# GNN pair kernel: layer 1 one group later, P ahead of K V, P turned through DRAM, five x slots

## The reference

```python
h = relu(layernorm(x))
z_l, z_g, v = h @ W_lang.T, h @ W_grav.T, h @ W_V.T
zn  = z_l / max(norm(z_l), 1e-8)
A_l = max(zn @ zn.T, 0) * not_eye
A_g = exp(-max(|z_g,n - z_g,m|^2, 0) / (2 sigma^2)) * not_eye
K   = w_l * rowstochastic(A_l * adj) + (1 - w_l) * rowstochastic(A_g * adj)
x   = x + (K @ v) @ W_O.T                 # layer 0
h   = relu(layernorm(x))
x   = x + einsum('bnf,nm->bmf', h, adj * adj) + bias   # layer 1
```

## Time and profile before

| | |
|---|---|
| median of 3 runs | 1266.11 us |
| profiled execution | 1266.65 us |
| its span, first to last instruction | 1264.8 us |
| mean granted TensorE clock | 0.994 |
| PE busy | 1241.4 us, 98% |
| DVE busy | 1058.7 us, 84% |
| ACT busy | 694.6 us, 55% |
| POOL busy | 575.5 us, 46% |

### The profile page before, as it was taken

One profiled execution on the slowest core, in us unless ns is written; L12 is line 12 of the kernel. 1 busy time (PEld: TensorE's weight loads), 2 busy tenths in 40 slices (PEclk: granted clock), 3 DMA queues, 4 the chain that ended last, 5 costly groups with the idle time before them and its releaser, 6 DMA issues.

```text
span 1264.8 us, 22572 instructions
## 1 busy us (share of the span) xinstructions
PE 1241.4 (98%) x6324; PEld 1039.9 (82%) x6324; DVE 1058.7 (84%) x1826; ACT 694.6 (55%) x1324; POOL 575.5 (46%) x964
## 2 busy tenths in 40 slices
PE   7999999999999999999999999999999999999996
PEld 7888888888888888888888888888888888888884
DVE  5688888898888898888898888898888898888777
ACT  6346655456655546655546655545655545664543
POOL 1124554434554434555444555444555343455433
PEclk9999999999999999999999999999999999999997
DMA  6233333443333444242444242444242334243201
GB/s 243 34 76 87 96 76 73 100 108 93 89 84 65 100 108 99 84 97 53 100 107 104 79 107 47 100 103 106 79 106 58 91 100 108 81 102 72 45 34 66
DMA packets 308894, 112.55 MB, mean 89 GB/s; under 512 B 269840, under 2 KB 269968, under 8 KB 308880
## 3 DMA queue, kind: packets, MB, share of 16 engines
q1 hardware_dynamic: 177360, 95.78, 27.6%
q10 hardware_dynamic: 131520, 16.60, 8.0%
HBM read 46.20 MB, written 33.62 MB: 63 GB/s over the span
## 4 chain that ended last, share of the span: by engine, by line
PE 92%; DVE 5%; issue 2%; ACT 1%; DMA 0%; DVEq 0%; ACTq 0%
PE ring L868 73%; PE p_ps L868 15%; PE p_ps L941 2%; PE kt_ps L881 1%; PE ring L958 1%; DVE x_out L689 1%; DVE y_lo L558 1%; PE p_ps L967 0%; DVE deg L603 0%; DMA x_ring<-in_L_gnn_W_lang 0%; DVE h L573 0%; DVE chain L587 0%; ACT v_hi L442 0%; DVE K L617 0%; ACT h L379 0%
## 5 line engine op out<-in xcount | busy, mean ns | idle before, releaser
L301 POOL TENSOR_TENSOR x_out<-x_ring,bias_sb 128x512 f32<-128x512 f32 x128 | 162.7, 1293 | 498.9 <-DVE bn L638 498.9
L406 ACT ACTIVATE y_hi<-ring 128x512 fp32r<-128x512 f32 x256 | 148.4, 593 | 201.8 <-PE ring L868 199.0
L868 PE MATMUL ring<-hT_hi,Lw_hi 128*128 128x512 f32 x640 | 256.4, 401 | 2.1 <-DVE hT_lo L577 1.3
L868 PE MATMUL ring<-hT_hi,Lw_lo 128*128 128x512 f32 x640 | 250.1, 391 | 0.0
L868 PE MATMUL ring<-hT_lo,Lw_hi 128*128 128x512 f32 x640 | 249.8, 390 | 0.0
L558 DVE TENSOR_TENSOR v_lo<-ring,v_hi 128x512 fp32r<-128x512 f32 x128 | 88.4, 692 | 137.2 <-ACT v_hi L442 137.2
L868 PE MATMUL ring<-MT_hi,hT_hi 128*128 128x512 f32 x512 | 202.6, 396 | 0.0
L868 PE MATMUL ring<-MT_lo,hT_hi 128*128 128x512 f32 x512 | 199.6, 390 | 0.0
L868 PE MATMUL ring<-MT_hi,hT_lo 128*128 128x512 f32 x512 | 199.6, 390 | 0.0
L308 POOL TENSOR_TENSOR h_lo<-h2f,h_hi 128x512 fp32r<-128x512 f32 x124 | 158.0, 1295 | 85.1 <-ACT h_hi L476 85.1
L558 DVE TENSOR_TENSOR y_lo<-ring,y_hi 128x512 fp32r<-128x512 f32 x256 | 168.8, 679 | 26.4 <-ACT y_hi L406 26.4
(11 more groups left out here) (160 smaller groups left out, 2539.6 us busy)
## 6 DMA issues: line engine op xcount, KB each, us to landing
x_ring<-in_x SPq DMA_DIRECT2D x32, 1024.0 KB, 5.5
out<-x_out SPq DMA_DIRECT2D x128, 256.0 KB, 2.2
h_turned<-h SPq DMA_DIRECT2D x248, 64.0 KB, 2.1
h_turned<-h ACTq DMA_DIRECT2D x248, 64.0 KB, 2.1
rn_cols<-rn_dram SPq DMA_DIRECT2D x31, 256.0 KB, 3.8
x_ring<-in_L_gnn_W_lang SPq DMA_DIRECT2D x4, 256.0 KB, 5.2
h2f<-in_L_gnn_W_grav SPq DMA_DIRECT2D x1, 1024.0 KB, 8.9
chain<-in_L_gnn_W_O SPq DMA_DIRECT2D x1, 1024.0 KB, 12.8
```

Of the source, the lines that this page charges most:

```text
L301: pool.tensor_tensor(x_out[:, b], x_rows(g, b), bias_sb[:, :], ALU.add).then_inc(x2b_ready, 1)
L406: act.activation(y[0][:, a, :, l], bank(n).rearrange("p (b m) -> p b m", b=GB), ACT.Copy)\
L868: mm = pe.matmul(out, lhsT, rhs, start=(k == 0), stop=(k == len(terms) - 1))
```

## The change

Diff line numbers are left out; "..." marks lines that are not shown. It does these things:

- P stands directly behind the y blocks and K's transposes, with its loop over a outside the loop over elements, and K V behind P. K's transposes stand behind the eighth y block instead of the seventh.
- The eight transposes of P on PE are gone, except in the last group. DVE transposes P's 32x32 blocks (`turn_p`, two operations), SP stores them to DRAM (two DMAs), and eight DMAs fetch them to their places in P_turned, which lies in the tile of h. S is then two adds in the next iteration (`sum_s`), behind the third y_lo, and mask, exponentials, row factors and the combination follow later in that iteration.
- The scaling by the norms and the mask are one operation on DVE; the product of spread norms and mask is made by POOL (`mask_norms`).
- Layer 1 of a group is computed an iteration later, with h2's hi and lo parts and the bias. x_out is gone: bias and output are added into x itself, which keeps five slots instead of four.
- All 16 DMAs of the turned h are issued by SP; ACT issues none in the loop. The second pair of block transposes stands behind the eighth y_lo.
- The statistics of the residual stand behind the lo parts of the first two elements of hT; all four `h2_full` stand at the end of ACT's iteration.

```diff
-SLOTS = 4
+SLOTS = 5
...
+            def store_p(g, l):
+                sp.wait_ge(p_blocks, 2 * g + l + 1)
+                sp.dma_start(p_dram[l], P_blocks[:, l].rearrange("p j b q -> p j (b q)")).then_inc(p_stored[l], 16)
+
+            def fetch_p(g, l):
+                sp.wait_ge(p_stored[l], 16 * g + 16)
+                for j in range(NQ):
+                    sp.dma_start(P_turned[j * Q:(j + 1) * Q, l], p_dram[l][:, j].rearrange("(i r) e -> r i e", r=Q))\
+                      .then_inc(p_turned[l], 16)
+
+            def spread_norms_turn_p(g):
                 sp.wait_ge(rn_step, RN_STEPS * g + 1)
                 sp.dma_start(rn_dram, rn[:, 0]).then_inc(rn_stored, 16)
                 sp.wait_ge(rn_stored, 16 * g + 16)
                 sp.dma_start(rn_cols[:, :, :], rn_dram.unsqueeze(0).to_broadcast([P, P, GB])).then_inc(rn_spread, 16)
+                store_p(g, 0)
+                store_p(g, 1)
+                fetch_p(g, 0)
+                fetch_p(g, 1)
 
             def turn_h(g):
                 sp.wait_ge(blocks_ready, GB * g)
-                for i in range(NQ // 2):
+                for i in range(NQ):
                     for j in range(NQ):
                         sp.dma_start(turned_to(i, j), h_blocks[i * Q:(i + 1) * Q, j]).then_inc(turned, 16)
 
-            def iteration(i, load=True, after=True):
-                if after:
-                    turn_h(i + 1)
-                if after:
-                    spread_norms(i)
-                store_out(i - 1, first_use(i) + PER - GB)
+            def iteration(i, load=True, lag=True):
                 if load:
-                    sp.wait_ge(x_loaded, 16 * i + 48)
-                    load_x(i + 3)
+
+                    sp.wait_ge(out_stored, 16 * GB * (i - 2))
+                    load_x(i + 2)
+                turn_h(i + 1)
+                spread_norms_turn_p(i)
+                if lag:
+                    store_out(i - 2, first_use(i) + PER - GB)
...
+            def mask_norms(g):
+                pool.wait_ge(rn_spread, 16 * g + 16)
+                pool.wait_ge(p_stored[0], 16 * g + 16)
+                by_row = mask[:, :].unsqueeze(1).to_broadcast([P, GB, P])
+                pool.tensor_tensor(rn_mask, rn_cols[:, :, :].rearrange("p m b -> p b m"), by_row, ALU.mult)\
+                    .then_inc(rn_masked, 1)
...
-            def iteration(i, before=True, after=True):
+            def iteration(i, before=True, lag=True, after=True):
                 if after:
                     norm1(i + 1)
+                if lag:
+                    for b in range(GB):
+                        h2_lo(i - 2, b)
+                    for b in range(GB):
+                        add_bias(i - 2, b)
+                row_norms(i)
                 if before:
-                    for b in range(GB // 2):
-                        add_bias(i - 1, b)
                     norm2(i - 1)
-                if not after:
-                    row_norms(i)
-                if before:
-                    for b in range(GB // 2, GB):
-                        add_bias(i - 1, b)
                 if after:
-                    row_norms(i)
-                if before:
-                    for b in range(GB):
-                        h2_lo(i - 1, b)
+                    mask_norms(i)
...
+                        act.wait_ge(s_ready, 2 * g - 2)
...
-            def turn_h(g):
-                act.wait_ge(blocks_ready, GB * g)
-                for i in range(NQ // 2, NQ):
-                    for j in range(NQ):
-                        act.dma_start(turned_to(i, j), h_blocks[i * Q:(i + 1) * Q, j]).then_inc(turned, 16)
 
...
-                        if after and 3 <= n < 5:
-                            normalize(i + 1, (n - 3) * GB // 2)
-                        if before and n == 4:
+                        if before and n == 3:
+                            exponentials(i - 1)
+                        if after and n == 5:
+                            normalize(i + 1, 0)
+                        if before and n == 6:
                             w_g_K_g(i - 1)
-                        if before and n == G_USES - 1:
-                            kt_copy(i - 1)
-                if after:
-                    turn_h(i + 1)
+                        if after and n == 7:
+                            normalize(i + 1, GB // 2)
+                if lag:
+                    for b in range(GB):
+                        h2_copy(i - 2, b)
+                if before:
+                    kt_copy(i - 1)
+                    act.wait_ge(s_ready, 2 * i)
+                for half in range(2):
+                    act.wait_ge(p_done, GB * i + 2 * half + 2)
+                    act.activation(P_sb[:, 2 * half:2 * half + 2], p_ps[:, 2 * half:2 * half + 2], ACT.Copy)\
+                       .then_inc(p_copied, 1)
+                if not after:
+                    shift(i)
...
-                    act.wait_ge(s_ready, i)
-                    act.wait_ge(diag_ready, 2 * i)
-                for half in range(2):
-                    act.wait_ge(p_done, GB * i + 2 * half + 2)
-                    act.activation(P_sb[:, 2 * half:2 * half + 2], p_ps[:, 2 * half:2 * half + 2], ACT.Copy)\
-                       .then_inc(p_copied, 1)
-                if not after:
-                    shift(i)
-                if before:
-                    h2_full(i - 1, 0)
-                    h2_full(i - 1, 1)
...
-                    if before and b == 0:
-                        h2_copy(i - 1, 0)
-                        h2_copy(i - 1, 1)
                     if b == 0 and after:
                         shift(i)
-                    if before and b == 1:
-                        h2_full(i - 1, 2)
-                    if before and b == 2:
-                        h2_full(i - 1, 3)
-                        h2_copy(i - 1, 2)
-                        h2_copy(i - 1, 3)
-                if after:
-                    exponentials(i)
+                if not after:
+                    kt_copy(i)
+                if before:
+                    for b in range(GB):
+                        h2_full(i - 1, b)
+                        if not after:
+                            h2_copy(i - 1, b)
...
             def mask_l(g):
-                dve.wait_ge(a_ready, 3 * g + 1)
+                dve.wait_ge(rn_masked, g + 1)
+                dve.wait_ge(s_ready, S_STEPS * (g + 1))
+                dve.scalar_tensor_tensor(out=A[:, :, 0], in0=A[:, :, 0], scalar=0.0,
+                                         in1=rn_mask,
+                                         op0=ALU.max, op1=ALU.mult).then_inc(a_ready, 1)
...
+            def output_bias(g, b, n):
+                dve.wait_ge(l1_done, GB * g + b + 1)
+                dve.wait_ge(h2_done, GB * g + b + 1)
+                dve.tensor_tensor(x_rows(g, b), x_rows(g, b), bias_sb[:, :], ALU.add).then_inc(x2b_last, 1)
+                dve.wait_ge(x2b_last, b + 1)
+                dve.tensor_tensor(x_rows(g, b), bank(n), x_rows(g, b), ALU.add).then_inc(drained, 1)
...
-                        if before and n == 1:
+                        if before and n == 3:
+                            sum_s(i - 1, 1)
+                            sum_s(i - 1, 0)
+                            mask_l(i - 1)
+                        if before and n == 4:
                             mask_g(i - 1)
-                        if before and n == 2:
                             row_factors(i - 1)
-                        if after and n == 4:
+                        if before and n == 6:
+                            combine(i - 1)
+                        if after and n == 6:
                             turn_blocks(i + 1, 0)
                             turn_blocks(i + 1, 1)
-                        if before and n == 4:
-                            combine(i - 1)
-                        if after and n == 5:
-                            turn_blocks(i + 1, 2)
-                            turn_blocks(i + 1, 3)
-                        if before and n == G_USES - 1:
-                            kt_lo(i - 1)
+                if after:
+                    turn_blocks(i + 1, 2)
+                    turn_blocks(i + 1, 3)
+                    if x_next:
+                        x_stats(i + 2, 0, GB)
+                if not after:
+                    last_chain(i, n, use, hi)
+                    return
                 if before:
-                    residual(i - 1, n, first_use(i) + n, i + 2 if stats and after else None)
+                    kt_lo(i - 1)
+                    add(i - 1, 0, n)
+                    add(i - 1, 1, n + 1)
+                squared_norms(i)
+                if before:
+                    add(i - 1, 2, n + 2)
+                    add(i - 1, 3, n + 3)
...
                     turned_lo(i + 1, b)
-                    if b == (2 if before else GB - 1):
-                        sum_s(i)
-                if before:
+                    if before and b < GB // 2:
```

(69 more changed lines are left out.)

## The result

The changed kernel takes **1283.53 us** (median of 4 runs, 1282.72 to 1283.90) against 1266.11: ratio 1.0136, 95% interval 1.0119 to 1.0154, slower by 1.4%. Its profiled execution took 1283.9 us with a span of 1282.1, clock 0.991.

A forecast was written before the change was run, and what follows sets the result against it. A ring of waits, 38.0 us a group, was taken to bound the changed kernel: 28 x 0.27 = 7.6, head 1.5, tail 4, so +13.1 us and 1279 us. Range 1248 to 1302, the forecast's own 1268 to 1292.

The forecast's parts named there:

- The ring: Loop's closed chain of waits through DVE, SP's DMAs, ACT and GpSimd: 38.0 us a group, 1.1 more than PE needs.
- the ends: Work outside the repeating groups: head +1.5 us (group 0's y to group 1's), tail +4 us behind the last K V.
- The transposes: Eight fp32 transposes of P on PE, removed in 31 of 32 groups: 0.87 us a group, leaving PE 36.86.
- rival 1: Turned h not late, TensorE stays the bound: 24.4 us go, ends cost 5.5, 1247 us, chance 0.16.
- (1): DVE from the first y_lo to the last block transpose: 13.3 us.
- (2): Turning h through 16 DMAs issued by SP alone, from turned blocks to turned h: 12.15 us.
- (3): ACT's hT_hi of the first element, behind the turned h: 0.62 us.
- (4): DVE's hT_lo, statistics, v_lo, second hT_lo and two more statistics: 4.3 us.
- (5): norm2 on GpSimd, from its first operation to the normalization it releases: 3.9 us.
- (6): Four h2f on ACT and the first y_hi, which releases the next y_lo: 3.45 us.
- six hand-overs of 0.05: Waits between the ring's steps, about 0.05 us each, added to their sum of 37.7 to give 38.0 us.
- rival 3: DVE's added strided operations and the fetches cost their upper ends: 38.9 us a group, 1304 us, chance 0.16.

The follow-up runs named there:

- h: Changed kernel with the residual's statistics two places earlier on DVE and GpSimd's product of norms and mask behind the next group's first norm: 1248.89 us.
- l: h with the last two block transposes also moved ahead of the eighth y_lo: 1245.93 us, ratio 0.9840.
- g: Old kernel without the turning of P (computes another matrix, only its time is of use): 1267.25 us, ratio 1.0008.
- d: Changed kernel with the last two block transposes ahead of the eighth y_lo: 1262.93 us, ratio 0.9977.
- e: Changed kernel with the last two block transposes behind the four statistics of x: 1370.97 us, ratio 1.0830.
- k: Changed kernel with six more small GpSimd multiplications ahead of the second norm's factors: 1340.01 us, ratio 1.0582.
- j: Changed kernel with only GpSimd's product of norms and mask moved behind the next group's first norm: 1282.78 us, ratio 1.0132.
- c: Changed kernel with only the residual's statistics moved two places earlier on DVE: 1286.20 us, ratio 1.0161.
- a: Changed kernel with ACT again issuing 8 of the 16 DMAs that turn h: 1267.37 us, ratio 1.0010.
- i: Changed kernel, last group only: GpSimd's factors ahead of its bias additions, each h_lo behind one output_bias on DVE: 1283.70 us, ratio 1.0141.
- section 4: Experiment on the changed kernel that moved statistics and mask product singly and together (c, j, h); its table lists landmark times from a group's first layer 1 output.

## Why the prediction came out right

It said 1279 us and slower; 1283.5 lies within the forecast's own range. The ring is shown by the runs. That the number came so close is in part luck, as the ends below tell.

**The transposes, 0.87 us a group: about right for PE, wrong as a gain that the old kernel could have taken.** The 36.86 us that I gave PE alone were passed in h and l (36.77 and 36.71, at 1248.9 and 1245.9 us). PE's busy time in a group fell by 1.16 us, from 37.68 to 36.52 in h, and not by 0.87: the V stage lost 0.93 us with the transposes, and the y stage 0.39 (14.14 to 13.75, means over groups 3 to 31), where I had put K's transposes and the new order at equal cost. That is rival 1, 1247 us, as a kernel: it needed the ring gone, as the text said. But g shows that in the old kernel nothing of it was to be had.

**The ring, step by step: confirmed.** From the rows above: (1) 573.39 to 586.65, 13.26 us, forecast 13.3. (2) to hT_hi at 598.88, 12.23, forecast 12.15. (3) 0.67, forecast 0.62. (4) 599.55 to 603.90, 4.35, forecast 4.3. (5) to 607.83, 3.93, forecast 3.9. (6) to the next y_lo at 611.28, 3.45, forecast 3.45. Sum 37.89, where the mean period is 37.88. My 38.0 came from six hand-overs of 0.05 put on top of 37.7; steps read from start to start held about half of them already. That is the term that was mis-sized: the loop lost 28 x 0.13 = 3.7 us and not 7.6. Runs d, e and k moved the period by 0.6, 3.1 and 1.9 us for 0.6, 2.4 and 1.7. GpSimd's product, put at nothing, did cost nothing in the changed kernel (j: 0.75 us for its move); c shows that only its place made it so.

**What I didn't see:** the twin ring over the first output and PE's y blocks, of the same length. It changes nothing in the forecast and everything in what one would do next. The prediction saw PE's stops as a result of the ring; they are part of the other one.

**Queues and adds.** SPq x16 in 10.72 us (said 10.6), no ACTq, hT_hi idle for 2.52 us behind the DMA (said 2), PE's stops of about 0.9 us. The strided adds cost 1.28 for two, dense, so rival 3 falls. The eight fetches took 3.65 us and nobody waited for them. The second queue by itself was worth 0.3 us a group (run a), far below the 4.97 us of issue that it takes off SP (10.72 to 5.75). The Trainium skill's rule ("DMA: Bandwidth & Descriptors", section Issuing engines are not separate DMA queues) that only initiating time is saved fits: from issue to landing a DMA takes 2.1 us with one queue and 2.2 with two. Its "usually small" does not fit, 10.72 us of issue for the 16 against 2.1.

**The ends: too small, +13.6 us in place of 5.5.** Group 0 to 1 was right (1.5). Groups 1 to 3 were not in the sum: layer 1 comes a group later, so group 1 has none, and PE has nothing between V and the late first y; it stands 5.00 us at 112.90 and then runs at the lower clock (granted 0.50 until 118, 0.63 us a matmul). This too is the late turned h: with it earlier the stop is 3.52 (d), 2.16 (a) and 2.20 us (l), and groups 1 to 3 take 77.6, 74.9 and 74.2 us in place of 79.4. The tail was +7.4 and not +4: beside the eight DVE operations that I counted, GpSimd's second factors start at 1269.28, behind a bias addition, but i shows that curing this queue brings nothing. What the missing 3.4 us are stays open.

The two errors, 3.9 too much in the loop and 8.1 too little at the ends, cancel in part: 17.3 us of span against 13.1. Most of the loss is at the ends, which the prediction gave less than half of it.

## What to carry to other kernels

Before an engine at 98% is relieved, look for the chain just below it: the old kernel had one of equal length (g), and the new one had two rings that tied, so that c and j by themselves showed a small loss and nothing, while the pair took 2.7% off; d paid alone, since it shortened both. Lengthen a ring as well as shorten it, and read landmarks relative to one event of the group, as in the table of section 4; a landmark that doesn't move names the other arm. When an operation of DVE or GpSimd moves, look at what the other engine does at that moment.

## What the runs showed of the hardware

DVE operations with two SBUF inputs and GpSimd operations that read SBUF stop each other in full: 0.68 to 1.97 us for DVE's hT_lo, 0.67 (in the old kernel) to 1.79 for its product with the selector in run a, and 0.20 to 0.69 for a small GpSimd addition (run k, 588.17, beside DVE's hT_lo). The mark of it is the end: in a, c, g and i the held DVE operation ends 0.54 to 0.56 us behind the end of the GpSimd operation that it met, however long it had stood. DVE's y_lo, which read one of their inputs from PSUM, kept their 0.60 us in h beside GpSimd's product (two from 592.67, beside 592.92). And one queue needs 0.67 us to issue each of these 64 KB DMAs, while two queues in run a needed 0.69 and 0.72 each at the same time: issuing from two engines at once is nearly free of mutual cost.
